# Reordered start of a layer kernel, and two attention answers given earlier in each batch

## The chip, the cores and the metric

The kernel runs on one core of a Trainium2 chip. The metric is the device time of one execution in microseconds (us). TensorE (PE in the profile) multiplies, VectorE (DVE), ScalarE (ACT) and GpSimd (POOL) do the elementwise work, and SyncE (SP) issues the DMAs. The engines run side by side and wait for each other only through semaphores.

## What is computed

```python
xn = _layernorm(x)                       # x: 4 batches x 2048 tokens x 256
# attention part, per batch
Q = l2norm(xn @ Wq.T + bq); K = l2norm(xn @ Wk.T + bk); V = xn @ Wv.T + bv
tailor = 1 / (L + Q^T (sum(K) + EPS))
s = xn + gamma * (sum(V) + Q^T (K V)) * tailor
# feed-forward part: both factors of every product are quantised to FP4, in blocks of 16
h = silu(q4(xn) @ q4(w_gate).T) * (q4(xn) @ q4(w_up).T)     # 704 wide
g = silu(q4(h) @ q4(w_down).T)
out = x + s * g
```

K, V and Q are never formed. The kernel builds the Gram matrix of the normalised rows of a batch, and from it, in a chain of small fp32 products, one 256 x 256 matrix M; s is then xn @ M.

## The kernel before

The 8192 rows go through in 32 pairs of 2 x 128 rows. The program of every engine is a start of its own, then the same iteration p = 0 to 32 written out (`drive`; the middle batches are a hardware loop), then a tail. In iteration p the engines work on different pairs at once. With u the pair number: `x_norm` (ACT) normalises pair u = p + 3 and writes its fp16 high part, `x_low` (POOL) writes the low part, `x_divide` (POOL) divides by the block scales; `x_abs` (ACT) and `x_round` (DVE) quantise pair p + 2; `row_transposes` (PE) and `rows_out` (ACT) turn pair p + 1 around; `gate_up` (PE), `silu` (ACT) and `h_mul` (DVE) form h of pair p in four pieces (j, c); `h_scales`, `h_abs`, `h_round` and others quantise h of pairs p and p - 1; `down_product` (PE) finishes pair p - 2. Ten iterations later PE multiplies the rows by M (`s_half`) beside all this.

The order on an engine is the order in which the calls are written; each call waits on its semaphores and whatever stands behind it waits too.

**The attention chain.** Three tables place its steps in the iterations of a batch: ASKS are PE's steps, ANSWERS are DVE's, COPIES are ACT's. A key is (i, j, place), where i counts the iterations of the batch and i = 0 is the iteration in which its last Gram product is formed. All PE steps write one PSUM bank, G. So the ask "gram1_0" at (0, 1, 2), the last thing that PE does in iteration i = 0, waits until the DVE answer "gram0" has emptied G; and the ask "high_low" at (5, 0, 1) waits until the answer "top" has computed the scalar kap. DVE gives "gram0" at (0, 1, 0), behind `h_round(0)`, `h_mul(1, 0)`, `x_round(2)` and `h_round(1)`, and "top" at (5, 0, 0), behind the first `h_mul` of iteration 5. The last batch has tables of its own (ASKS_END and so on).

**The start.** The gate, up and down weights are quantised in three units z = 0, 1, 2 by the same means as the rows: DVE takes the block maxima, POOL divides (`w_divide`, L485), ACT takes the absolute value (`w_abs`), DVE rounds (`w_round`, L1132 and L1138) and multiplies by the high and by the low scales (`w_scaled`, L1145, two fp16 instructions of up to 128 x 1536; the second raises `wlod`). PE then turns unit 0 and unit 1 around (`gate_up_weights`, 11 steps), ACT copies them out (`gate_up_out`), and only after the eleventh copy can `gate_up` of iteration 0 begin. Unit 2 is scaled in iteration 0 and turned in iterations 0 and 1 (`down_transposes`, L1348; `down_out`, L812). Pairs 0, 1 and 2 are normalised and quantised in between. Their transposes for the later product with M are `first_rows(0)` and `first_rows(1)` in the start and part of `row_transposes` in iteration 0. "weights_v" sums the columns of Wv on PE (four fp32 products, L1568) and ACT copies the sum (L605).

In the start POOL's order is: x_rstd, x_low of pair 0, w_divide(0), x_divide of pair 0, w_divide(1), x_rstd and x_low of pair 1, w_divide(2), x_divide of pair 1, x_rstd and x_low of pair 2, x_rstd of pair 3, x_divide of pair 2.

In every iteration ACT does `x_norm(p)` before `silu(p, 0, 0)`.

Of the kernel before, what the change touches and what calls it, by code (L numbers as in the profile page):

```python
# [26 lines left out]
F16 = mybir.dt.float16  # L27
BF16 = mybir.dt.bfloat16

P = 128  # L30
# [40 lines left out]
def build(nc, x, Wq, bq, Wk, bk, Wv, bv, gamma, w_gate, w_up, w_down, out):  # L71
# [3 lines left out]
    with ExitStack() as ctx:  # L75
# [178 lines left out]
        def spread_in_order(ap, blks):  # L254
# [5 lines left out]

        ASKS = {(-2, 1, 2): "gram0_0", (-1, 0, 1): "gram0_1", (-1, 1, 1): "gram0_2", (6, 1, 2): "gram0_0", (0, 0, 1): "gram0_3",
                (0, 1, 2): "gram1_0", (1, 0, 0): "gram1_1", (1, 0, 2): "turn", (2, 0, 0): "t1q", (2, 0, 2): "t1k",
                (2, 1, 2): "norms", (3, 0, 2): "raw", (3, 1, 2): "tailor", (4, 0, 2): "product", (4, 1, 2): "top",
                (5, 0, 1): "high_low"}
        ANSWERS = {(0, 1, 0): "gram0", (1, 0, 1): "gram1", (1, 1, 0): "turn", (2, 1, 0): "squares",
                   (3, 0, 0): "norms", (4, 0, 0): "tailor", (4, 0, 3): "scale", (4, 1, 0): "product", (5, 0, 0): "top", (5, 0, 2): "high_low"}
        COPIES = {(2, 0, 1): "t1q", (3, 1, 0): "raw"}

# [187 lines left out]
        def _(pool):  # L456
# [62 lines left out]
            x_rstd(-2)  # L519
            x_low(-2, 0)  # L520
            w_divide(2)
            x_divide(-2, 0)
            x_rstd(-1)
            x_low(-1, 1)
            x_rstd(0)
            x_divide(-1, 1)
# [53 lines left out]
        def _(act):  # L580
# [16 lines left out]
            def copy(b, step):  # L597
                matrices = G[:, :].rearrange("p (k n) -> p k n", k=KD)
                if step in ("weights_q", "weights_k"):
                    i = int(step == "weights_k")  # L600
                    act.wait_ge(S["a_tr"], i + 1)
                    a.copy((wqT, wkT)[i][:, :, :], matrices).then_inc(S["a_ev"], 1)
                if step == "weights_v":
                    act.wait_ge(S["wvs_mm"], 1)
                    a.copy(wvs[:, :], G[:, 0:D]).then_inc(S["wvs_ev"], 1)  # L605
                if step == "t1q":
                    wait(act, "tq_mm", b + 1)
                    a.copy(t1q[:, :, :], matrices).then_inc(S["tq_ev"], 1)
                if step == "raw":
                    wait(act, "inv_d", b + 1)  # L610
                    wait(act, "raw_mm", b + 1)
                    for m in range(KD):
                        last = a.activation(raw[:, m], matrices[:, m], ACT.Copy, scale=inv[:, 2 + m:3 + m])
                    last.then_inc(S["raw_ev"], 1)
# [152 lines left out]

            def first_rows_out(u):
                for j in range(2):
                    act.wait_ge(S["n_tr"], 2 * u + j + 1)  # L770
                    xn_out(u, j, "n_ev")

            act.wait_ge(S["consts"], 3)
# [13 lines left out]
            w_abs(1)  # L787
            own_basis(1)
            first_rows_out(0)
            copy(0, "weights_q")  # L790
            for r in range(GUR):
                gate_up_out(r)
                if r == 3:
                    x_stats(-1)
                if r == R0 - 1:
                    copy(0, "weights_k")
                    w_abs(2)
                    x_high(-2, 0)
                    x_norm(-1, 1)
                    x_stats(0)  # L800
                    first_rows_out(1)
                if r == R0 + 2:
                    x_abs(-1, 1)
            for j in range(2):
                rows_out(-1, 1, j, False, False)
            copy(0, "weights_v")
            x_high(-1, 1)

# [6 lines left out]
            def iteration(p, k, b=0, i=-1, tail=False):  # L815
# [7 lines left out]
                if i == 3:  # L823

                    wait(act, "gram_d", 2 * b + 2)
                if on["xa"]:
                    x_norm(p, k)
                if on["m"]:
                    silu(p, 0, 0)
                attention(0, 0)  # L830
                down_out(p, 0, 0)
# [469 lines left out]
        def _(pe):  # L1301
# [13 lines left out]
            t.matmul(DS[:, 0:2], ones32[0:2, :], wdiag[:, :], start=True, stop=True).then_inc(S["walld"], 1)  # L1315
            def first_rows(u):
                for j in range(2):
                    pe.wait_ge(S["xhi"], u + 1)
                    pe.wait_ge(S["xlo"], u + 1)

                    wait(pe, "n_ev", 2 * u - 1 + j)
                    norm_transposes(u, j).then_inc(S["n_tr"], 1)

            def gate_up_weights(r):
# [56 lines left out]
            def row_transposes(p, k, j, h_on, n_on):  # L1381
# [9 lines left out]
                if isinstance(p, int) and p == -1:  # L1391
                    pe.wait_ge(S["n_ev"], 4)
                for z in range(4):
# [76 lines left out]
            def ask(b, step):  # L1470
# [81 lines left out]
                if step in ("weights_q", "weights_k"):  # L1552
# [7 lines left out]
                    for k in range(KD):  # L1560
                        for n in range(KD):
                            last = t.transpose(G[:, k * D + n * P:k * D + (n + 1) * P], wqkv[:, w, n, k * P:(k + 1) * P], id32[:, :])
                    last.then_inc(S["a_tr"], 1)
                if step == "weights_v":
                    pe.wait_ge(S["a_ev"], 2)
                    pe.wait_ge(S["w_own"], 2)
# [3 lines left out]

            first_rows(0)
            ask(0, "weights_q")
            for r in range(R0):
                gate_up_weights(r)
            first_rows(1)
            ask(0, "weights_k")
            for r in range(R0, GUR):
                gate_up_weights(r)
            for j in range(2):
                row_transposes(-1, 1, j, False, False)  # L1580
            ask(0, "weights_v")

# [82 lines left out]
```

## Time and profile before

| | |
|---|---|
| time, median of 3 runs | 608.24 us (607.51 to 609.05) |
| profiled execution: its own time | 607.78 us |
| its span, first to last instruction | 605.7 us |
| DVE busy | 559.3 us, 92% |
| PE busy | 549.9 us, 91% |
| ACT busy | 416.0 us, 69% |
| POOL busy | 246.6 us, 41% |
| mean granted TensorE clock | 0.983 |

The table comes from the page of the profiled execution. DVE and PE share the load almost evenly, so a share of busy time does not say which of them holds the end back in a given stretch; that is read from who waits for whom. In a timeline a row has its start, its length, the engine, line and operation, what it writes and reads, and how often; several instructions of one kind in a row are merged. A bracket gives the idle time before it and what ended that.

### The profile page before, as it was taken

What the parts mean: (1) busy time and instruction counts of PE and PEld (TensorE: products, weight loads), DVE (VectorE), ACT (ScalarE), POOL (GpSimd) and SP (SyncE); (2) the same over time, 40 slices, a digit from 0 to 9 for tenths busy, and PEclk for the clock granted to TensorE, in tenths of its full rate; (3) what the DMA queues carried; (4) which work ended last, traced back from release to release, by engine and by line L of the source; (5) the groups of instructions that cost most, each with busy time, mean ns of one, the idle gap of its engine ahead of it and who ended that gap; (6) DMA issues with size and microseconds to landing.
All of it is one profiled execution on the core that took longest, in us unless ns stands there. A gap on an engine that the chain in (4) does not pass through costs nothing. (4 is left out here: it accounts for less than half of the span.)

```text
span 605.7 us, 15173 instructions
## 1 busy us (share of the span) xinstructions
PE 549.9 (91%) x4957; PEld 427.4 (71%) x4957; DVE 559.3 (92%) x1178; ACT 416.0 (69%) x902; POOL 246.6 (41%) x214
## 2 busy tenths in 40 slices
PE   0478899999999999899999989989999999999886
PEld 0345576768776877678887767768887777778775
DVE  7988999999999999989999997999999999987873
ACT  4878788867787777656876767767777677545331
POOL 7533333333342334444442543444243444423136
PEclk9969899999999999989999999999999999999999
DMA  7010000000011001111011111110111111013033
GB/s 247 17 27 28 19 19 18 18 19 19 18 36 36 18 2 54 55 54 52 3 54 54 54 57 55 53 36 20 54 53 54 55 36 37 36 49 124 22 122 140
DMA packets 17488, 29.14 MB, mean 48 GB/s; under 512 B 2688, under 2 KB 4864, under 8 KB 17408
## 3 DMA queue, kind: packets, MB, share of 16 engines
q1 hardware_dynamic: 17408, 28.13, 14.0%
q8 instruction: 44, 0.72, 0.5%
q14 instruction: 36, 0.29, 0.2%
HBM read 19.73 MB, written 8.39 MB: 46 GB/s over the span
## 5 line engine op out<-in xcount | busy, mean ns | idle before, releaser
L1416 PE MATMUL GU<-wgu,xqT 128*128 128x352 f16 x1536 | 254.8, 317 | 5.5 <-DVE h L935 3.1
L1416 PEld LDWEIGHTS GU<-wgu,xqT 128*128 128x128 f16 x1536 | 149.2, 99 | 80.6 <-issue 4.7
L622 ACT ACTIVATE sil<-GU,wkap 128x352 f32<-128x352 f32 x128 | 70.8, 553 | 71.3 <-PE GU L1416 70.3
L541 POOL TENSOR_TENSOR ht<-h,hrr 128x1408 f32<-128x1408 f32 x32 | 82.9, 2589 | 82.5 <-DVE hrr L949 81.0
L1426 PE MATMUL DS<-wdT,hqT 128*128 128x256 f16 x704 | 87.3, 273 | 1.9 <-ACT hqT L629 1.9
L935 DVE SCALAR_TENSOR_TENSOR h<-GU,wkap,sil 128x352 f32<-128x352 f32 x128 | 69.4, 542 | 18.8 <-ACT sil L622 17.6
L504 POOL TENSOR_TENSOR xnat<-xs,xnat 128x510 f16<-128x510 f32 (+1 forms) x32 | 38.7, 1209 | 106.8 <-DVE hq L983 96.7
L983 DVE TENSOR_TENSOR hq<-hg,hs 128x704 f16<-128x704 f16 x128 | 78.9, 657 | 0.9
L1426 PEld LDWEIGHTS DS<-wdT,hqT 128*128 128x128 f16 x704 | 66.7, 98 | 12.0 <-ACT hqT L629 2.3
L494 POOL TENSOR_TENSOR rs<-ve,half 128x2 f32<-128x2 f32 x32 | 23.9, 747 | 114.3 <-DVE ht L972 109.4
L658 ACT ACTIVATE gring<-DS,hun 128x256 f32<-128x256 f32 (+1 forms) x64 | 29.9, 467 | 43.6 <-issue 29.6
L629 ACT COPY hqT<-TR 128x768 f16<-128x768 f16 x64 | 50.9, 796 | 8.4 <-PE TR L1378 7.4
L972 DVE SCALAR_TENSOR_TENSOR ht<-hT,ht 128x1408 f32<-128x1408 f32 x32 | 51.8, 1619 | 2.4 <-ACT hT L671 2.1
L1428 PE MATMUL DS<-wdT,hqT 128*128 128x256 f16 x384 | 52.4, 273 | 0.0
L975 DVE SCALAR_TENSOR_TENSOR hg<-hT,ht 128x1408 f16<-128x1408 f32 x32 | 51.7, 1616 | 0.0
L942 DVE TENSOR_REDUCE ham<-h 128x88 f32<-128x1408 f32 x32 | 51.4, 1607 | 0.0
L1378 PE MATMUL TR<-id,hq 128*128 128x128 f16 x704 | 50.5, 221 | 0.5 <-DVE hq L983 0.5
L511 POOL TENSOR_TENSOR xt<-xs,xrr 128x512 f32<-128x512 f32 x32 | 34.0, 1061 | 37.0 <-DVE hq L983 25.2
L1437 PE MATMUL GU<-Mx,xnT 128*128 128x128 f16 (+1 forms) x552 | 47.7, 223 | 0.0
L1437 PEld LDWEIGHTS GU<-Mx,xnT 128*128 (+1 forms) x552 | 39.7, 98 | 9.6
L1378 PEld LDWEIGHTS TR<-id,hq 128*128 128x128 f16 x704 | 43.4, 99 | 3.3 <-DVE hq L983 1.1
L671 ACT ACTIVATE hT<-ht 128x1408 f32<-128x1408 f32 x32 | 43.8, 1369 | 1.7 <-POOL ht L541 1.3
(163 smaller groups left out, 955.3 us busy)
## 6 DMA issues: line engine op xcount, KB each, us to landing
xin<-in_L_attn_x SPq DMA_DIRECT2D x34, 256.0 KB, 2.8
xe<-in_L_attn_x SPq DMA_DIRECT2D x25, 256.0 KB, 2.8
out<-o SPq DMA_DIRECT2D x25, 256.0 KB, 2.1
algebra<-in_L_ffn_w_down SPq DMA_DIRECT2D x1, 704.0 KB, 6.7
gring<-in_L_ffn_w_up SPq DMA_DIRECT2D x1, 640.0 KB, 5.5
xs<-in_L_attn_x SPq DMA_DIRECT2D x2, 256.0 KB, 4.1
xt<-in_L_attn_x SPq DMA_DIRECT2D x2, 256.0 KB, 4.5
out<-xin SPq DMA_DIRECT2D x2, 256.0 KB, 2.5
```

Of the source, the lines that this page charges most:

```text
L541: g.tensor_tensor(paired(ht[:, 0:2 * I]), paired(h[:, q]), spread(hrr[:, q], 4 * CB), ALU.mult).then_inc(S["ht_d"], 1)
L622: a.activation(sil[:, c], GU[:, c, 0, 0:CH], ACT.Silu, scale=wkap[:, 0:1]).then_inc(S["sil_d"], 1)
L935: v.scalar_tensor_tensor(h[:, k, (2 * j + c) * CH:(2 * j + c + 1) * CH], GU[:, c, 1, 0:CH], wkap[:, 0:1], sil[:, c], ALU.mult, ALU.mult).t ...
L942: v.tensor_reduce(per_block(ham[:, :]), paired_in_order(h[:, q]), AX.X, ALU.max, apply_absolute_value=True).then_inc(S["ham_d"], 1)
L972: v.scalar_tensor_tensor(ht[:, 0:2 * I], hT[:, 0:2 * I], CUT, ht[:, 0:2 * I], ALU.max, ALU.subtract).then_inc(S["hw_d"], 1)
L975: v.scalar_tensor_tensor(hg[:, 0:2 * I], hT[:, 0:2 * I], CUT, ht[:, 0:2 * I], ALU.max, ALU.subtract).then_inc(S["hg_d"], 1)
L983: v.tensor_tensor(paired(hq[:, q, j, at:at + I]), paired(hg[:, j * I:(j + 1) * I]), spread(scales[:, q, j * HB:(j + 1) * HB], HB), ALU.mul ...
L1378: last = t.transpose(TR[:, bank, zz * P:(zz + 1) * P], hq[:, q, j, z * P:(z + 1) * P], id16[:, :])
L1416: last = t.matmul(GU[:, c, m, 0:CH], xqT[:, k, j, 2 * a_ + kc], wgu[:, b_, kc, 2 * m + c], start=(z == 0 and kc == 0), stop=(z == 2 and kc ...
L1426: t.matmul(DS[:, 0:D], hqT[:, j, z], wdT[:, z], start=(z == 0), stop=False)
L1428: last = t.matmul(DS[:, 0:D], hqT[:, j, LOCH + z], wdT[:, NCH + z], start=False, stop=(z == LOCH))
L1437: last = t.matmul(bank, slot[:, j, 2 * a_ + kc], Mb[:, b_, kc, columns], start=(i == 0 and kc == 0), stop=(i == 2 and kc == KD - 1))
```

## The change

- POOL: the third weight division, w_divide(2), first waits until the scaled copies of unit 0 are written (`wlod` at 1). x_low of pairs 1 and 2 goes behind a wait for the last weight rounding (`wgd` at 3), with x_divide of pair 2 behind them.
- PE and ACT: the eight transposes of pair 1 for the product with M and their copy leave the start, become a step "rows_1" that uses the bank G, and are done in iteration 0; "weights_v" leaves the start too, asked at the end of iteration 0 and copied in iteration 1.
- ACT: x_high of pair 2 moves from the end of the start into iteration 0, behind the first silu. In iterations 0 and 1 `silu(p, 0, 0)` comes before `x_norm(p)`.
- DVE, batches 0, 1 and 2: the answer "gram0" moves from (0, 1, 0) to (0, 0, 3), ahead of `h_round(0)`; the answer "top" (kap) from (5, 0, 0) to (4, 1, 2), between `h_scales(0)` and `h_scales(1)` of the iteration before.

```diff
-        ASKS = {(-2, 1, 2): "gram0_0", (-1, 0, 1): "gram0_1", (-1, 1, 1): "gram0_2", (6, 1, 2): "gram0_0", (0, 0, 1): "gram0_3",
+        ASKS = {(-5, 0, 1): "rows_1", (-5, 1, 1): "weights_v", (-2, 1, 2): "gram0_0", (-1, 0, 1): "gram0_1", (-1, 1, 1): "gram0_2", (6, 1, 2): "gram0_0", (0, 0, 1): "gram0_3",
...
-        ANSWERS = {(0, 1, 0): "gram0", (1, 0, 1): "gram1", (1, 1, 0): "turn", (2, 1, 0): "squares",
-                   (3, 0, 0): "norms", (4, 0, 0): "tailor", (4, 0, 3): "scale", (4, 1, 0): "product", (5, 0, 0): "top", (5, 0, 2): "high_low"}
-        COPIES = {(2, 0, 1): "t1q", (3, 1, 0): "raw"}
+        ANSWERS = {(0, 0, 3): "gram0", (1, 0, 1): "gram1", (1, 1, 0): "turn", (2, 1, 0): "squares",
+                   (3, 0, 0): "norms", (4, 0, 0): "tailor", (4, 0, 3): "scale", (4, 1, 0): "product", (4, 1, 2): "top", (5, 0, 2): "high_low"}
+        COPIES = {(-5, 1, 0): "rows_1", (-4, 0, 1): "weights_v", (2, 0, 1): "t1q", (3, 1, 0): "raw"}
...
             w_divide(1)
             x_rstd(-2)
-            x_low(-2, 0)
+
+            pool.wait_ge(S["wlod"], 1)
             w_divide(2)
             x_divide(-2, 0)
             x_rstd(-1)
+            x_rstd(0)
+
+            pool.wait_ge(S["wgd"], 3)
+            x_low(-2, 0)
             x_low(-1, 1)
-            x_rstd(0)
             x_divide(-1, 1)
...
+                if step == "rows_1":
+                    act.wait_ge(S["n_tr"], 3)
+                    a.copy(xnT[:, 1], G[:, :].bitcast(F16).rearrange("p (j z t) -> p j z t", j=2, t=P)).then_inc(S["n_ev"], 1)
...
-                    first_rows_out(1)
...
-            copy(0, "weights_v")
-            x_high(-1, 1)
...
-                if on["xa"]:
+                first = isinstance(p, int) and p < 2
+                if on["xa"] and not first:
                     x_norm(p, k)
                 if on["m"]:
                     silu(p, 0, 0)
+                if isinstance(p, int) and p == 0:
+                    x_high(-1, 1)
+                if on["xa"] and first:
+                    x_norm(p, k)
...
+                if step == "rows_1":
+                    pe.wait_ge(S["a_ev"], 2)
+                    pe.wait_ge(S["xhi"], 2)
+                    pe.wait_ge(S["xlo"], 2)
+                    for j in range(2):
+                        for z in range(4):
+                            last = t.transpose(G[:, :].bitcast(F16)[:, (4 * j + z) * P:(4 * j + z + 1) * P],
+                                               xnat[:, 1, j, z * P:(z + 1) * P], id16[:, :])
+                    last.then_inc(S["n_tr"], 1)
                 if step == "weights_v":
-                    pe.wait_ge(S["a_ev"], 2)
+                    pe.wait_ge(S["n_ev"], 3)
...
-            first_rows(1)
             ask(0, "weights_k")
...
-            ask(0, "weights_v")
```

## Rows read from the trace of the kernel before

**Rows 1.** The page: busy time, share and instructions of each engine

```profile
PE 549.9 (91%) x4957; PEld 427.4 (71%) x4957; DVE 559.3 (92%) x1178; ACT 416.0 (69%) x902; POOL 246.6 (41%) x214
```

**Rows 2.** Timeline of VectorE, start to iteration 1

```profile
19.97 1.21 DVE L1124 SCALAR_TENSOR_TENSOR ws<-y,wall,ws 128x96 f16<-128x96 f32 x1
21.28 4.03 DVE L1145 TENSOR_TENSOR xnat<-hg,ws 128x1536 f16<-128x1536 f16 x2
...
44.92 0.58 DVE L935 SCALAR_TENSOR_TENSOR h<-GU,wkap,sil 128x352 f32<-128x352 f32 x1 [1.99 <-ACT sil L622]
...
57.86 0.58 DVE L935 SCALAR_TENSOR_TENSOR h<-GU,wkap,sil 128x352 f32<-128x352 f32 x1 [1.75 <-ACT sil L622]
...
62.43 1.61 DVE L972 SCALAR_TENSOR_TENSOR ht<-hT,ht 128x1408 f32<-128x1408 f32 x1
```

**Rows 3.** Source line L1145, unit 0 and 2: shortest, median, longest, ns

```profile
L1145 DVE TENSOR_TENSOR xnat<-hg,ws x4: 857/914/3162, 21.3 to 47.1; 128x1536 f16<-128x1536 f16 x2, 128x1408 f16<-128x1408 f16 x2
```

**Rows 4.** Timeline of GpSimd in the start

```profile
18.72 2.35 POOL L504 TENSOR_TENSOR xnat<-xs,xnat 128x510 f16<-128x510 f32 x1 [2.59 <-ACT xnat L724]
21.02 2.60 POOL L485 TENSOR_TENSOR ht<-algebra,y 128x1408 f32<-128x1408 f32 x1
26.61 1.06 POOL L511 TENSOR_TENSOR xt<-xs,xrr 128x512 f32<-128x512 f32 x1 [2.98 <-DVE xrr L906]
```

**Rows 5.** Timeline of ScalarE, iterations 0 and 1

```profile
42.70 1.09 ACT L711 ACTIVATE xs<-xin,x_shift,rs 128x256 f32<-128x256 f32 x2
...
49.10 2.10 ACT L812 COPY wdT<-TR 128x1024 f16<-128x1024 f16 x3 [0.91 <-PE TR L1348]
...
58.40 0.56 ACT L622 ACTIVATE sil<-GU,wkap 128x352 f32<-128x352 f32 x1
...
60.70 1.39 ACT L671 ACTIVATE hT<-ht 128x1408 f32<-128x1408 f32 x1
```

**Rows 6.** Timeline of TensorE: "gram1_0" of batches 1 and 2, "high_low" of 1

```profile
255.45 1.99 PE L1486 MATMUL G<-xnat 128*128 x8 [2.54 <-DVE algebra L1019]
257.24 3.57 PE L1416 MATMUL GU<-wgu,xqT 128*128 128x352 f16 x12
...
334.57 0.66 PE L1550 MATMUL G<-id,mt 128*128 128x128 f32 x4 [0.84 <-DVE kap L1067]
...
396.96 1.88 PE L1486 MATMUL G<-xnat 128*128 x8 [1.61 <-DVE algebra L1019]
```

**Rows 7.** Timeline of TensorE, end of the start and iterations 0 and 1

```profile
37.04 2.02 PE L1568 MATMUL G<-wqkv,ones 128*128 128x256 f32 x4
38.85 5.32 PE L1416 MATMUL GU<-wgu,xqT 128*128 128x352 f16 x24
...
50.32 1.95 PE L1416 MATMUL GU<-wgu,xqT 128*128 128x352 f16 x12
...
54.52 1.95 PE L1416 MATMUL GU<-wgu,xqT 128*128 128x352 f16 x12
```

**Rows 8.** Who VectorE waited for, 255 to 300 us (batch 1)

```profile
DVE h L935 <- ACT sil L622: 2.9, 4, 1.0
```

**Rows 9.** Who VectorE waited for, 396 to 440 us (batch 2)

```profile
DVE h L935 <- ACT sil L622: 1.4, 3, 0.7
```

**Rows 10.** Who VectorE waited for, 120 to 160 us (batch 0)

```profile
DVE ht L972 <- ACT hT L671: 0.6, 1, 0.6
```

**Rows 11.** Who VectorE waited for, 355 to 375 us

```profile
DVE h L935 <- ACT sil L622: 2.5, 1, 2.5
```

**Rows 12.** Windows: busy time by engine, granted TensorE clock, DMA share, GB/s

```profile
32.00:42.00 10.00, 8.06 (x43) 5.81 (x44) 9.72 (x16) 6.47 (x17) 3.07 (x3) 0.50 0.11 29
42.00:52.00 10.00, 7.36 (x63) 4.92 (x62) 7.87 (x21) 7.20 (x17) 3.94 (x5) 1.00 0.10 26
```

**Rows 13.** Timeline of VectorE where "gram0" is answered, batch 1

```profile
249.71 1.62 DVE L972 SCALAR_TENSOR_TENSOR ht<-hT,ht 128x1408 f32<-128x1408 f32 x1
...
254.37 0.41 DVE L1015 TENSOR_SCALAR algebra<-G 128x256 f32<-128x256 f32 x1
```

More of the change, by code:

```diff
@@ L766, in w_kappa @@
                 a.activation(wkap[:, 1:2], wbeta[:, 1:2], ACT.Copy, scale=-1.0 / (HTOP * TIE * TIE)).then_inc(S["wkapd"], 1)
[L768 to L771, printed above, removed]
             act.wait_ge(S["consts"], 3)
@@ L788, in _ @@
             own_basis(1)
-            first_rows_out(0)
+            for j in range(2):
+                act.wait_ge(S["n_tr"], j + 1)
+                xn_out(0, j, "n_ev")
             copy(0, "weights_q")
@@ L1315, in _ @@
             t.matmul(DS[:, 0:2], ones32[0:2, :], wdiag[:, :], start=True, stop=True).then_inc(S["walld"], 1)
[L1316 to L1322, printed above, removed]
             def gate_up_weights(r):
@@ L1391, in row_transposes @@
                 if isinstance(p, int) and p == -1:
-                    pe.wait_ge(S["n_ev"], 4)
+                    pe.wait_ge(S["n_ev"], 2)
                 for z in range(4):
@@ L1563, in ask @@
                     last.then_inc(S["a_tr"], 1)
+                if step == "rows_1":
+                    pe.wait_ge(S["a_ev"], 2)
+                    pe.wait_ge(S["xhi"], 2)
+                    pe.wait_ge(S["xlo"], 2)
+                    for j in range(2):
+                        for z in range(4):
+                            last = t.transpose(G[:, :].bitcast(F16)[:, (4 * j + z) * P:(4 * j + z + 1) * P],
+                                               xnat[:, 1, j, z * P:(z + 1) * P], id16[:, :])
+                    last.then_inc(S["n_tr"], 1)
                 if step == "weights_v":
-                    pe.wait_ge(S["a_ev"], 2)
+                    pe.wait_ge(S["n_ev"], 3)
                     pe.wait_ge(S["w_own"], 2)
@@ L1569, in ask @@
                     last.then_inc(S["wvs_mm"], 1)
-            first_rows(0)
+            for j in range(2):
+                pe.wait_ge(S["xhi"], 1)
+                pe.wait_ge(S["xlo"], 1)
+                norm_transposes(0, j).then_inc(S["n_tr"], 1)
             ask(0, "weights_q")
```

## The prediction

> **What bounds the kernel.** I first read the page. VectorE is busy for 92% of the span and TensorE for 91% [rows 1], so the bound has to be found stretch by stretch. The waits of VectorE do that: where it waits for nothing, its own work sets the end; where it waits for a silu, the chain through TensorE does. The timelines of the start and then of a whole batch show four places that matter to this change.
>
> In the start, VectorE reaches the two scaled copies of weight unit 0 at 21.28 and needs 4.03 us for them [rows 2]. Their single durations are 857 to 914 ns, and one of them takes 3162 ns [rows 3]. GpSimd ran x_low of pair 1 from 18.72 to 21.07 and the third weight division from 21.02 to 23.62 [rows 4]. So VectorE stood still until GpSimd's instruction was over. The small one before them, 96 elements wide, took 1.21 us from 19.97 [rows 2], nearly all of it the tail of x_low.
>
> Between the start and iteration 0, VectorE waits 1.99 us for the first silu [rows 2], since ScalarE put x_norm (from 42.70) in front of it [rows 5]. After the 1.75 us wait at 57.86 [rows 2] VectorE is never short of work for about a hundred us, so what the start wins on VectorE by its first large rounding of h, at 62.43 [rows 2], should last.
>
> In each batch TensorE stops for the answer "gram0". In batch 1 it stops 2.54 us and in batch 2 1.61 us [rows 6]. After the stop of batch 1 the next 12 products take 3.57 us where 12 take 1.95 elsewhere [rows 6, 7]: the clock has dropped. VectorE then waits 2.9 us for silus [rows 8]. In batch 2 it waits 1.4 us [rows 9], in batch 0 0.6 us [rows 10]. After "high_low" TensorE stops for kap, 0.84 us in batch 1 [rows 6], and the next wait of VectorE is 2.5 us at the turn of the hardware loop [rows 11].
>
> **The start, part by part.** *The scaled copies.* With x_low moved away and the division waiting, GpSimd is idle there. The copies return 4.03 less two of 0.9, that is 2.2; the small one returns about 0.9 of its 1.21 (at most the 1.10 in which x_low overlapped it). Unit 0 is ready at 22.2 instead of 25.3, 3.1 earlier.
>
> *What comes behind it.* The third division, 2.60 long, now starts at 22.2 and ends at 24.8; x_divide of pair 1 (1.06, [rows 4]) follows and runs to 25.9. VectorE arrives at the rounding of unit 1 at about 25.0, an instruction that reads two tiles like those that stood still, and I charge it 0.9. If only some kinds of instruction stand still, the charge is 0. I take 0.9, as the row of x_low is the nearest. That leaves 2.1 for unit 1. The Trainium skill (SBUF — State Buffer, "Who interferes with whom") says that a VectorE instruction with two SBUF inputs and a GpSimd instruction that reads SBUF exclude each other for the whole instruction, and that whoever issues first wins. The 3162 ns of the blocked copy agree. By that rule the 0.9 is a real charge and the rule speaks against this order; were the two to share instead, the start would win some 0.5 more.
>
> *Up to iteration 0.* ScalarE loses the two copies for pair 1, and TensorE loses weights_v, which held it for 2.02 us from 37.04, right in front of the first gate_up at 38.85 [rows 7]. With the 2.1 this lets gate_up begin at about 35.2. Its first half takes 3.5 us at the low clock that this stretch has (0.50, [rows 12]), so the silu is done at 39.4. VectorE is through with its start at 40.2 instead of 42.9: the 2.1, and 0.7 since the x_low of pair 2 no longer blocks a rounding. The 1.99 us wait goes. The first h_mul comes at 40.2, 4.7 earlier.
>
> *What is late next.* The two x_low start when the last weight rounding is done, at about 39.1, and take 2.3, then x_divide of pair 2 runs to 42.4. Behind x_low on ScalarE stands x_norm of pair 3, behind x_divide stands x_abs of pair 2, and behind that the second silu, at 43.1. VectorE comes to the scaled copies of unit 2 at 41.6 and stands until 42.4: 0.8 is given back. 3.8 is left.
>
> *rows_1.* Eight transposes on TensorE (0.45 at full clock, by the spacing of those merged rows elsewhere) and a copy of 1024 elements on ScalarE. The three copies of the down weights took 2.10 [rows 5], so one of the large ones is about 0.95. It stands in front of the copies of the down weights, which TensorE waits for before gate_up(0, 1, 1). That one starts at 47.2 instead of 50.32 [rows 7]: 3.1 is left.
>
> *weights_v.* Four products, 2.02 at half clock [rows 7, 12], so 1.0 at full clock, in front of gate_up(1, 0, 0): 52.3 plus nothing else, instead of 54.52 [rows 7]. 2.2 is left.
>
> *The silu ahead of the norm in iteration 1.* ScalarE is free from 52, but now its first task is a silu that can't start before 54.3. x_norm and its two casts (1.6 in all, of which 1.09 is the norm itself [rows 5]) follow it, then x_abs, then silu(1, 0, 1) at 57.05 instead of 58.40 [rows 5]. The copy of weights_v adds 0.3, so h_abs goes from 60.70 [rows 5] to 59.65 and VectorE's rounding from 62.43 to 61.05. **The start wins 1.4.** Bounds: 3.8 if none of what follows iteration 0's first half is on VectorE's path, 0 if one more of these blockings or copies lands on it.
>
> **The batches.** *gram0.* Its two instructions (0.41 and a like one) move ahead of four units of work that begin at 249.71, to be compared with 254.37 [rows 13]. They are done at 250.6. TensorE comes to the ask at 252.9 (255.45 less 2.54, [rows 6]), so no wait is left, with 2.3 to spare. The move itself costs VectorE nothing, as the instructions are the same; it makes one h_mul 0.8 later, whose reader on TensorE is two pieces away. TensorE gains 2.54 and the 1.62 of the slow twelve in batch 1, more than the 2.9 that VectorE waited: all 2.9 is won. In batch 2 the stop is 1.6, more than the 1.4: all 1.4. In batch 0 at most 0.6, and I take it. Lower bounds: TensorE could use up its lead before the waits come, and 0 is won.
>
> *kap.* It is ready 0.84 earlier, and nothing lies between it and the loop's turn for which TensorE waits: 0.8 of the 2.5 there. In batches 0 and 2 VectorE waits for nothing afterwards, so 0. The answer comes behind the large reduction, 1.6 us after TensorE has delivered its input, so it adds no wait. Bounds 0 and 2.5.
>
> Sum: 1.4 + 2.9 + 1.4 + 0.6 + 0.8 = 7.1. The profiled execution took 607.8 in its own time (span 605.7), which gives 600.7. The median of the runs stands 0.4 above it, so 601.1, with 598.5 to 603.5 as this case's own range.
>
> **The rivals.** *A, the whole start is kept* (3.8 instead of 1.4): 598.7. For it: VectorE hardly waits in iteration 0. Against it: TensorE and ScalarE, not VectorE, set gate_up(1, 0, 0).
>
> *B, the stops of TensorE cost nothing where they are removed.* It then meets another limit of its own, and VectorE waits as before. Batches 1 and 2 return at most 1 together: 605.8. For it: TensorE is 100% busy in both stretches, so part of the waits may be its work and not its lateness. Against it: batch 1 had the longer stop and the longer waits.
>
> *C, B with nothing won in the start either*: 607.5, no change.
>
> *D, slower: the low clock lasts.* The clock was at its lower level, 1.2 GHz (0.50), from 32 to 42 and at full level after that [rows 12]. TensorE had been idle from 29 to 33 us, and was busy almost without a break from 36 on when it rose. In the new order it is idle from about 26.3 to 30.2 and has short breaks up to 35.2. If the rise comes later, each gate_up of 12 products costs 3.57 instead of 1.95 [rows 6, 7], 1.6 each, on the chain. It decides from the fifth of these on, 8 us against the 7.1. Seven of them, up to about 60 us, give 612.4. Against it: gate_up now begins 3.6 earlier and gives an unbroken run of 24 products as before. The Trainium skill (TensorE: Matmul & The Clock Gate, "Why this matters for your kernels") warns of idle gaps between bursts of products; the 3.57 [rows 6] agree.
>
> **How the numbers follow.** Forecast 0.52, A 0.16, B 0.17, C 0.08, D 0.07. A difference under 0.3%, 1.8 us, can't be told from none. Faster: the forecast, A and nearly all of B, 0.83. Same: C and the rest of B, 0.10. Slower: D, 0.07. The range goes from 597.8, beyond A by the wider bound of kap, to 606.2, which takes in B.
>
> **What would show it.** The copies of L1145 all at about 0.9 for unit 0; the rounding of unit 1 (L1132, 1280 wide) at 2.3 or so instead of 1.5; the first h_mul near 40; a wait of ScalarE for gate_up before the first silu of iteration 1; the h rounding near 61. Later, no stop of TensorE at gram1_0 and no clock drop behind it, no waits of VectorE for silus in the first iterations behind gram0 of batches 1 and 2, and 1.7 instead of 2.5 at the loop's turn. The prediction is wrong if those waits stay although the stop is gone, or if the clock rises well after 42.

## The result and the profile after

The changed kernel takes 601.77 us (median of 4 runs, 599.99 to 601.82), the kernel before 608.64 on the same chip (4 runs, 607.51 to 609.33). The ratio is 0.988, with a 95% interval of 0.9864 to 0.9897. Forecast were 601.1 us, 597.8 to 606.2 and a chance of 0.83 for faster. The profiled execution took 601.82 us, with a span of 599.7, 6.0 shorter than before.

In this kernel the lines have moved: the scaled copies are L1151, the roundings of the weights L1138 and L1144, `h_mul` L941, the rounding of h L978, `silu` L629, `x_norm` L718, `gate_up` L1414.

The page again first, for the busy times that answer to [rows 1]:

```profile
PE 549.6 (92%) x4957; PEld 426.0 (71%) x4957; DVE 557.2 (93%) x1178; ACT 416.1 (69%) x901; POOL 258.9 (43%) x214
```

VectorE is busy for 2.1 us less. An instruction that another engine holds up counts as busy while it stands still, so the shorter copies of the start are in this. The other 3.9 of the 6.0 us are waiting of VectorE that has gone. To see where, follow one instruction that stands once in each iteration through both traces: VectorE's large reduction of h (128x1408), L942 before and L948 after. It appears 32 times, the last at 569.17 before and 561.64 after. Its start before less its start after is what has been won up to there; such a list is called a ledger below:

| the reduction of | time before | won up to there | what lies since the row above |
|---|---|---|---|
| pair 0 | 53.5 | 3.4 | the start |
| pairs 1 to 5 | 69.9 to 128.4 | 1.6, at the last 1.5 | iterations 0 and 1 |
| pairs 7 to 13 | 161.4 to 258.3 | 2.8 to 3.0 | "gram0" of batch 0 |
| pair 15 | 295.7 | 6.05 | "gram0" of batch 1 |
| pair 21 | 399.8 | 5.8 | kap of batch 1, turn of the loop |
| pair 23 | 435.5 | 7.4 | "gram0" of batch 2 |
| pair 31 | 569.2 | 7.5 | the last batch |
| end of the span | 605.7 | 6.0 | the tail |

The start, on VectorE's timeline, to be held against [rows 2]:

```profile
20.24 0.32 DVE L1130 SCALAR_TENSOR_TENSOR ws<-y,wall,ws 128x96 f16<-128x96 f32 x1
20.66 1.83 DVE L1151 TENSOR_TENSOR xnat<-hg,ws 128x1536 f16<-128x1536 f16 x2
...
25.29 2.23 DVE L1138 SCALAR_TENSOR_TENSOR h<-gring,h 128x1280 f32<-128x1280 f32 x1
...
39.95 0.48 DVE L941 SCALAR_TENSOR_TENSOR h<-GU,wkap,sil 128x352 f32<-128x352 f32 x1
...
41.30 2.44 DVE L1151 TENSOR_TENSOR xnat<-hg,ws 128x1408 f16<-128x1408 f16 x2
...
54.61 0.58 DVE L941 SCALAR_TENSOR_TENSOR h<-GU,wkap,sil 128x352 f32<-128x352 f32 x1 [1.91 <-ACT sil L629]
...
60.79 1.63 DVE L978 SCALAR_TENSOR_TENSOR ht<-hT,ht 128x1408 f32<-128x1408 f32 x1 [0.37 <-ACT hT L678]
```

And GpSimd's, against [rows 4]:

```profile
22.57 2.60 POOL L485 TENSOR_TENSOR ht<-algebra,y 128x1408 f32<-128x1408 f32 x1 [6.16 <-DVE xnat L1151]
25.11 1.07 POOL L511 TENSOR_TENSOR xt<-xs,xrr 128x512 f32<-128x512 f32 x1
...
38.90 2.27 POOL L504 TENSOR_TENSOR xnat<-xs,xnat 128x510 f16<-128x510 f32 x2 [6.44 <-DVE hg L1144]
41.12 1.07 POOL L511 TENSOR_TENSOR xt<-xs,xrr 128x512 f32<-128x512 f32 x1
```

Read the two together. The copies of unit 0 now take 1.83 instead of 4.03, and the division starts as they end. The rounding at 25.29 takes 2.23; where GpSimd is quiet it takes 1.47 (below). The division has ended at 25.17, so what it stands beside is L511, x_divide of pair 1, from 25.11 to 26.18. The copies of unit 2, at 41.30, take 2.44 where two take 1.6 to 1.7, and reach their normal speed when L511 ends at 42.19. These are the 0.9 and the 0.8 of the prediction. The first h_mul stands at 39.95 with no wait before it. Then VectorE meets waits of 1.91 and 1.04 for silus, and the rounding of h comes at 60.79, 1.6 earlier than before.

TensorE in the middle of batch 1, against [rows 6]:

```profile
254.01 1.80 PE L1484 MATMUL G<-xnat 128*128 x8
255.66 1.95 PE L1414 MATMUL GU<-wgu,xqT 128*128 128x352 f16 x12
...
260.84 0.66 PE L1493 MATMUL G<-id,algebra 128*128 128x128 f32 x4 [0.59 <-DVE algebra L1025]
```

The stop at the Gram product is gone, and so is the slow group of twelve (1.95 instead of 3.57). VectorE has no wait for a silu any more in the stretches of [rows 8, 9] and no wait at all in that of [rows 10]. TensorE now waits 0.6 for the next answer, "turn", which stands where it stood.

At the turn of the hardware loop the view of VectorE's waits, 352 to 375 us, against [rows 11]:

```profile
DVE h L941 <- POOL ht L545: 2.8, 1, 2.8
DVE h L941 <- issue: 0.4, 1, 0.4
```

And the tail, on TensorE's timeline and in the windows of TensorE alone (busy time, granted clock, DMA share, GB/s):

```profile
567.34 0.38 PE L1543 MATMUL G<-mtop,ones 128*128 128x1 f32 x2 [1.45 <-DVE mtop L1068]
568.17 1.11 PE L1548 MATMUL G<-id,mt 128*128 128x128 f32 x4 [0.45 <-DVE kap L1073]
569.08 2.52 PE L1424 MATMUL DS<-wdT,hqT 128*128 128x256 f16 x11
```

```profile
566.00:568.00 2.00, 0.38 (x2) 1.00 0.00 0
568.00:570.00 2.00, 1.83 (x9) 0.50 0.00 0
570.00:572.00 2.00, 2.00 (x14) 0.64 0.75 251
```

The groups of twelve and of eleven products that this text follows are always the same ones, so their length shows the clock. After two idle times of TensorE, 1.45 and 0.45 us, the clock falls to its lower level, 1.2 GHz (0.50), and eleven products take 2.52 instead of 1.36. The kernel before had the same idle times at 575 us and kept its clock there:

```profile
574.87 0.38 PE L1545 MATMUL G<-mtop,ones 128*128 128x1 f32 x2 [1.45 <-DVE mtop L1062]
...
576.20 1.36 PE L1426 MATMUL DS<-wdT,hqT 128*128 128x256 f16 x11
```

So the tail gives back 1.5 of the 7.5.

### The profile page after: what moved, and what is told of

It is laid out like the page before. It is cut to its first block and busy times, and to the rows that moved or that the text cites. A ratio compares the mean times of both kernels' runs of the same rounds, so it can differ in the third digit from the quotient of the medians.

```text
span 599.7 us, 15172 instructions
## 1 busy us (share of the span) xinstructions
PE 549.6 (92%) x4957; PEld 426.0 (71%) x4957; DVE 557.2 (93%) x1178; ACT 416.1 (69%) x901; POOL 258.9 (43%) x214
## 5 line engine op out<-in xcount | busy, mean ns | idle before, releaser
L1414 PE MATMUL GU<-wgu,xqT 128*128 128x352 f16 x1536 | 252.6, 315 | 5.5 <-DVE h L941 2.1
L1414 PEld LDWEIGHTS GU<-wgu,xqT 128*128 128x128 f16 x1536 | 148.3, 99 | 79.7 <-issue 3.6
L629 ACT ACTIVATE sil<-GU,wkap 128x352 f32<-128x352 f32 x128 | 70.8, 554 | 59.8 <-PE GU L1414 58.9
L941 DVE SCALAR_TENSOR_TENSOR h<-GU,wkap,sil 128x352 f32<-128x352 f32 x128 | 69.2, 540 | 13.6 <-ACT sil L629 9.7
L504 POOL TENSOR_TENSOR xnat<-xs,xnat 128x510 f16<-128x510 f32 (+1 forms) x32 | 37.0, 1159 | 89.9 <-DVE hq L989 81.6
L978 DVE SCALAR_TENSOR_TENSOR ht<-hT,ht 128x1408 f32<-128x1408 f32 x32 | 51.8, 1619 | 1.9 <-ACT hT L678 1.9
L948 DVE TENSOR_REDUCE ham<-h 128x88 f32<-128x1408 f32 x32 | 51.5, 1608 | 0.0
L511 POOL TENSOR_TENSOR xt<-xs,xrr 128x512 f32<-128x512 f32 x32 | 34.0, 1063 | 26.6 <-DVE hq L989 25.1
```

Of the source, the lines that this page charges most:

```text
L629: a.activation(sil[:, c], GU[:, c, 0, 0:CH], ACT.Silu, scale=wkap[:, 0:1]).then_inc(S["sil_d"], 1)
L941: v.scalar_tensor_tensor(h[:, k, (2 * j + c) * CH:(2 * j + c + 1) * CH], GU[:, c, 1, 0:CH], wkap[:, 0:1], sil[:, c], ALU.mult, ALU.mult).t ...
L948: v.tensor_reduce(per_block(ham[:, :]), paired_in_order(h[:, q]), AX.X, ALU.max, apply_absolute_value=True).then_inc(S["ham_d"], 1)
L978: v.scalar_tensor_tensor(ht[:, 0:2 * I], hT[:, 0:2 * I], CUT, ht[:, 0:2 * I], ALU.max, ALU.subtract).then_inc(S["hw_d"], 1)
L1414: last = t.matmul(GU[:, c, m, 0:CH], xqT[:, k, j, 2 * a_ + kc], wgu[:, b_, kc, 2 * m + c], start=(z == 0 and kc == 0), stop=(z == 2 and kc ...
```

## The experiments

Twelve kernels ran, each beside the kernel before on the same chip; medians of the kernel before were 608.34, 608.75 and 609.18 in the three groups. Where a reading rests on one profile, it is of one execution. The start differs from profile to profile: VectorE's second rounding of weight unit 0, the last instruction ahead of everything that was changed, stands at 17.89 to 19.11. It is at 18.31 in the kernel before and at 18.59 in the change; "shift" below is measured by it. What is won after iteration 1 varies too among profiles with the same order of the start: 0, -0.1, -0.3 and -0.7 for the old one, 1.4, 1.5, 1.6 and 1.8 for the new one. So a single difference there is good to some 0.4 us.

### One part of the change at a time

*gram0_only*: the kernel before with

```diff
-        ANSWERS = {(0, 1, 0): "gram0",
+        ANSWERS = {(0, 0, 3): "gram0",
```

> The kernel before with one edit: the answer gram0 at (0, 0, 3). Theory (the stops of TensorE at gram1_0 were on VectorE's path, as the waits behind them say): VectorE's large reductions shift by 1.2 us in batch 0, 3.2 more in batch 1 and 1.6 more in batch 2, so the last of them comes 6.0 earlier and the time is 602 to 603, ratio near 0.990; if TensorE's clock drops in the tail as it did in the profile of the changed kernel, 1.6 of it goes back. Rival (the start's shift is what made room): well under 4 us earlier, with waits for silus left in batches 1 and 2.

*top_only*: the kernel before with `(4, 1, 2): "top"` instead of `(5, 0, 0): "top"`.

> The kernel before with one edit: the answer top (kap) at (4, 1, 2). The prediction's term: 0.8 us earlier at the turn of the hardware loop. Theory now: 0, since both traces show VectorE's 2.5 to 2.8 us there ending long after the silu was there; the wait is its own queue's, and TensorE's earlier arrival buys nothing. TensorE's stop for kap (0.84) should be gone in either case.

*start_only*: the changed kernel with both answers put back, which leaves all the edits of the start.

> The changed kernel with both answers back where they were: only the start differs from the kernel before. Theory: the large reduction of iteration 1 comes 1.6 us earlier and the shift stays 1.6 to the end, time 606 to 607. Rival (predicted case A): up to 3.4, since the reduction of iteration 0 came 3.4 earlier. Rival (C): no change.

| | median, us | ratio, 95% | won at the last large reduction | span |
|---|---|---|---|---|
| gram0_only | 602.22 (6 runs) | 0.9909 [0.9889, 0.9928] | 5.8 | 599.8 |
| top_only | 607.78 (12 runs) | 0.999 [0.9978, 1.0002] | 1.5 | 604.1 |
| start_only | 606.11 (12 runs) | 0.9966 [0.9956, 0.9976] | 3.5 | 603.9 |

gram0 alone brings 6.1 us by the medians, the start 2.2, and the 0.6 of top_only can't be told from none, as its interval reaches 1.0002. In gram0_only the winnings come in three steps, 1.2 in batch 0, 3.2 in batch 1, 1.6 in batch 2, the same as in the whole change. In start_only they are 1.8 after iteration 1; the rest, 1.65, appears in batch 1, where this edit does nothing. There the profile of before has a drop of the clock [rows 6] that the profile of start_only hasn't. top_only shows the same jump at the same place (from -0.5 to 1.1). All three ledgers hold this 1.65, and it is the profile of before that has the drop; so of the 3.2 of batch 1 only about 1.6 is the stop itself. This also settles the sum: 5.8, 1.5 and 3.5 make 10.8, and with the 1.65 counted once instead of three times 7.5, which is what the whole change wins up to the same row. That the drop comes in some executions of one kernel and not in others is likely, but no kernel was profiled both with and without it.

What kap does at the loop's turn is seen in the waits of top_only, VectorE 350 to 375 us:

```profile
DVE h L935 <- PE GU L1437: 2.5, 1, 2.5
DVE h L935 <- issue: 0.4, 1, 0.4
```

The stop of TensorE for kap has gone, and the wait at the loop's turn is the same 2.5 to the tenth. At its own place the move does win a little: the ledger of top_only goes up by 0.13, 0.20 and 0.17 at the reductions of pairs 10, 18 and 26, 0.5 in all, where those of gram0_only and start_only go up by at most 0.02. In batch 1 the time from the reduction to the second h_mul behind it is 4.77 instead of 4.95, with no wait in either: the two instructions of kap cost VectorE less behind the reduction than between two h_muls.

### The order of the start

*no_wait_third_division*: the changed kernel without the first wait.

```diff
-            pool.wait_ge(S["wlod"], 1)
             w_divide(2)
```

> The changed kernel without POOL's wait for the scaled copies of unit 0 ahead of the third weight division; x_low of pairs 1 and 2 stay late. Theory: the division then runs from about 16.4 to 19.0, beside the rounding of unit 0 (two tiles read, f32), and the scaled copies at 20.7 meet no GpSimd instruction: the wait buys nothing, the copies take 1.8 as in the changed kernel, though one rounding of unit 0 may be blocked for up to 1 us. Time within 1 us of the changed kernel. Rival (the wait is what freed the copies): the copies take about 4 again and unit 0 is ready 2 us later, up to 1 us of it in the time.

Measured: 602.72 (4 runs), ratio 0.9902 [0.9885, 0.9919]. The theory fell and the rival's time came. VectorE:

```profile
18.12 1.74 DVE L1143 SCALAR_TENSOR_TENSOR hg<-hT,ht 128x1536 f16<-128x1536 f32 x1
...
20.20 4.08 DVE L1150 TENSOR_TENSOR xnat<-hg,ws 128x1536 f16<-128x1536 f16 x2
...
27.09 1.47 DVE L1137 SCALAR_TENSOR_TENSOR h<-gring,h 128x1280 f32<-128x1280 f32 x1
```

GpSimd, the same stretch:

```profile
15.82 0.20 POOL L497 TENSOR_TENSOR x_shift<-nm,rs 128x2 f32<-128x2 f32 x1
20.01 2.59 POOL L485 TENSOR_TENSOR ht<-algebra,y 128x1408 f32<-128x1408 f32 x1 [3.98 <-DVE hg L1143]
```

GpSimd is done at 16.0 and the division starts at 20.01, when VectorE's second rounding (hg<-hT,ht) is over. The wait before it is not GpSimd being held up: the division writes the tile ht which that rounding reads, and `w_divide(2)` has a wait of its own for it (`wgd` at 1). The expectation had left this wait out. So the division can't come before the copies, only beside them or behind them. Beside them it holds them up, 4.08 for the two, as in [rows 2]; this agrees with the Trainium skill (SBUF — State Buffer, "Who interferes with whom"), that the one that starts first keeps the shared ports for its whole instruction. The rounding of unit 1 is then free, 1.47, but the h rounding comes at 61.80 instead of 60.79, although this profile has its second rounding of unit 0 0.5 earlier. By the profiles the wait in front of the third division is worth 1.0 to 1.5 us. The ratios alone don't show it, as the interval here and that of the change, 0.9864 to 0.9897, overlap; the medians give 0.8.

*wait_alone*: the kernel before with that one line in front of w_divide(2), and x_low(-2, 0) still ahead of it.

> The kernel before with one edit: POOL waits for the scaled copies of unit 0 before the third weight division, x_low of pair 1 stays ahead of it. Theory: the small copy of scales still takes 1.2 (x_low), the scaled copies 1.8 instead of 4.0, and the whole start 2 us earlier there, of which ScalarE's queue and the low clock keep part: 0.5 to 1.5 us off the time. Rival: another thing sets the start's end (transposes of pair 1, weights_v, x_norm ahead of the silu): under 0.3 us.

Measured: 607.04 (12 runs), 0.9974 [0.9962, 0.9985]; 1.7 us by the medians, a little above the 0.5 to 1.5 expected. Its profile wins 0.3 after iteration 1, 0.8 with its shift of 0.47 taken out. The copies take 1.83, but x_low still stretches the instruction before them, which takes 1.21 as in [rows 2], and the first silu is waited for as before, 1.99. Removing the line and adding it both say that it carries a good part of what the start wins. The other edits of the start (x_low behind the roundings, the transposes of pair 1, x_high, the silu first in iteration 0) were not tried one by one.

*norm_first_in_1*: the changed kernel with the old order in iteration 1, x_norm ahead of the silu.

```diff
-                first = isinstance(p, int) and p < 2
+                first = isinstance(p, int) and p < 1
```

> The changed kernel with the silu ahead of the norm in iteration 0 only; in iteration 1 x_norm comes first again. Theory (ScalarE sits idle 1.7 us before that silu and then has x_norm, 1.6 us, on the path to silu(1, 0, 1) and h_abs): the norm fills the idle time and the rounding of h comes about 1 us earlier than the 60.8 of the changed kernel; the time is about 1 us lower than its 601.8. Rival: the silu is what VectorE waits for and the order of the change is right: the same or up to 1 us higher.

*weights_v_later*: the changed kernel with "weights_v" asked at (-4, 1, 1) and copied at (-3, 0, 1), an iteration later.

> The changed kernel with weights_v asked one iteration later, at the end of iteration 1, and copied in iteration 2. Theory (its four products, 1.08 us on TensorE, stand in front of gate_up(1, 0, 0), which ScalarE and then VectorE wait for): the first silu of iteration 1 comes 0.9 us earlier, h_abs about 1.1 earlier, the rounding of h at about 60.0 instead of 60.8, time 0.8 lower than the changed kernel's. Rival: another wait replaces it, under 0.3.

| | median, us | ratio, 95% | gate_up(1, 0, 0) | h rounding |
|---|---|---|---|---|
| the change | 601.77 (4 runs) | 0.988 [0.9864, 0.9897] | 52.03 | 60.79 |
| norm_first_in_1 | 599.34 (5 runs) | 0.9851 [0.9834, 0.9868] | | 60.36 |
| weights_v_later | 599.22 (5 runs) | 0.9848 [0.9831, 0.9865] | 51.16 | 59.63 |

Both medians lie 2.4 to 2.6 below the change's, more than the 1.0 and 0.8 expected. But three of the change's four executions probably have the clock drop of the tail, and neither of these two profiles has it; against filler_in_tail below (600.14), which is the change without that drop, they are 0.8 and 0.9 lower. The ledgers at the last reduction say 8.5 and 9.0 instead of 7.5. norm_first_in_1 is shifted by 0.52 against the change, so its rounding is 0.9 earlier, not 0.4; weights_v_later is shifted by 0.05. ScalarE in norm_first_in_1:

```profile
52.72 1.09 ACT L718 ACTIVATE xs<-xin,x_shift,rs 128x256 f32<-128x256 f32 x2
...
54.52 0.55 ACT L629 ACTIVATE sil<-GU,wkap 128x352 f32<-128x352 f32 x1
...
56.37 0.56 ACT L629 ACTIVATE sil<-GU,wkap 128x352 f32<-128x352 f32 x1 [0.61 <-PE GU L1414]
```

ScalarE in the change:

```profile
54.02 0.56 ACT L629 ACTIVATE sil<-GU,wkap 128x352 f32<-128x352 f32 x1 [1.70 <-PE GU L1414]
54.48 1.08 ACT L718 ACTIVATE xs<-xin,x_shift,rs 128x256 f32<-128x256 f32 x2
```

In the change ScalarE stands idle for 1.70 before the silu and then does x_norm; with the norm first that idle time is filled, and the second silu waits for TensorE and not for the norm. This edit of the change costs about 0.9 in iteration 1. "weights_v" costs 0.9 at gate_up(1, 0, 0), and 1.2 at the rounding, as its copy of 0.37 stands in front of h_abs too.

### The clock drops

*filler_in_tail*: the changed kernel with eight products that nothing reads, in the last batch, behind the last h_mul and ahead of the wait for "top". They add work and change no result.

```diff
+                    if isinstance(b, int) and b == BATCHES - 1:
+                        pe.wait_ge(S["h_d"], 4 * PAIRS)
+                        for z in range(8):
+                            t.matmul(GU[:, 0, 0, 0:CH], xqT[:, 0, 0, 0], wgu[:, 0, 0, 0], start=True, stop=True)
```

> The changed kernel with eight products of 352 columns, whose result nobody reads, ahead of TensorE's wait in the ask top of the last batch, where it idles 1.45 us. Theory (the half clock at 568 to 571 us in the changed kernel's profile, 1.6 us, follows from that idle time and hits some executions only): the clock stays at full level there, and the median falls by up to 1.6 us to about 600.2. Rival: the drop has another origin or was in this one profile alone, the time stays.

Measured: 600.14 (599.47 to 600.30, 5 runs), 0.9854 [0.9839, 0.9868]. TensorE:

```profile
565.66 1.36 PE L1545 MATMUL GU<-wgu,xqT 128*128 128x352 f16 x8
567.28 0.38 PE L1547 MATMUL G<-mtop,ones 128*128 128x1 f32 x2 [0.26 <-DVE mtop L1068]
568.11 0.66 PE L1552 MATMUL G<-id,mt 128*128 128x128 f32 x4 [0.45 <-DVE kap L1073]
568.60 1.36 PE L1424 MATMUL DS<-wdT,hqT 128*128 128x256 f16 x11
```

The idle time of 1.45 is down to 0.26, the clock stays at 1.00 and the eleven products take 1.36. The profile keeps all of its 7.6: the span is 598.1. The five times lie within 0.9 us of each other and at least 1.4 below the three slower ones of the change, as the theory had it.

*filler_at_gram1*: the kernel before, gram0 not moved, with ten such products between the two groups of Gram products in batches 0 to 2, where TensorE waits for "gram0".

```diff
+                    if part == 0 and m == 1 and not (isinstance(b, int) and b == BATCHES - 1):
+                        wait(pe, "g_d", 2 * PB * b + 8)
+                        for z in range(10):
+                            t.matmul(DS[:, D:2 * D], wgu[:, 0, 0, 0, 0:P], wgu[:, 0, 0, 1, 0:D], start=True, stop=True)
```

> The kernel before with ten products of 256 columns, whose result nobody reads, in TensorE's stop ahead of gram1_0 in batches 0, 1 and 2; it first waits for ScalarE's last read of that bank. Theory (of the 3.2 us that batch 1 won in the profile, 1.6 was a clock drop that follows from the stop and hits only some executions): the stop stays, filled, the slow twelve products don't appear, and the profile is up to 1.6 shorter than the kernel before's. Rival: all 3.2 is the stop, nothing changes.

Measured: 608.33 (606.34 to 609.82, 10 runs), 0.9982 [0.9968, 0.9997]. The drop in batch 1 is gone:

```profile
254.53 1.26 PE L1481 MATMUL DS<-wgu 128*128 128x256 f16 x10 [0.71 <-ACT gring L658]
256.38 1.83 PE L1490 MATMUL G<-xnat 128*128 x8 [0.58 <-DVE algebra L1019]
258.07 1.96 PE L1416 MATMUL GU<-wgu,xqT 128*128 128x352 f16 x12
```

and VectorE's wait there, 255 to 300 us, has halved against [rows 8]:

```profile
DVE h L935 <- ACT sil L622: 1.4, 3, 0.7
```

1.5 of the 2.9 was the slow clock, 1.4 the stop. The ledger of this profile shows 1.7 won in batch 1, 0.6 lost in batch 0, where there was no drop to prevent, and a drop in the tail (eleven products in 2.51) that costs 1.5. So the profile is 0.8 longer than the one of before and not shorter, and the median gains 0.9, with an interval that ends at 0.9997. Filling the stop is no substitute for moving the answer.

How often do the drops come? Of the 12 profiles of this case without the filler in the tail, 5 have slow products there (2.52, 2.51, 2.43, 2.35 and 1.97 instead of 1.36): the change and its repetition, start_only, both_in_1 and filler_at_gram1. The kernel before, gram0_only, top_only, wait_alone and three others have none, with the same idle times in front. Both the old and the new order of the start stand on both sides, so no edit explains it. The drop in batch 1 is like it: of the four profiles that have gram0's stop unfilled and unmoved, the kernel before and wait_alone (twelve products in 3.57 and 3.35) have it, start_only and top_only (1.96 each) don't, with stops of 2.53 to 2.56 in all four.

### The better versions, and the change once more

*both_in_1*: the changed kernel with norm_first_in_1 and weights_v_later together.

> The changed kernel with both improvements of iteration 1: x_norm ahead of the silu again, and weights_v one iteration later. Theory: with weights_v gone the silu is ready at 53.1 while the norm would hold ScalarE to 54.0, so most of what the two won alone is the same time on ScalarE; the rounding of h comes at about 59.4, 0.2 to 0.3 earlier than with weights_v moved alone, time about 599.0. Rival: they add up, 1.9 lower than the changed kernel in the profile.

*both_and_filler*: both_in_1 with the filler in the tail.

> The same with the eight unread products ahead of TensorE's wait in the ask top of the last batch. Theory: the clock doesn't drop in the tail in any execution; the median is up to 1.6 lower than without where the drop hits most executions, about 598, and the runs lie closer together. Rival: other drops take its place and the two are the same.

*changed_once_more*: the change itself.

> The changed kernel itself once more, for the spread of its executions: the theory of the tail's clock drop expects two groups, near 600.0 without and near 601.8 with it.

| | median, us | ratio, 95% | h rounding | won at the last reduction | span |
|---|---|---|---|---|---|
| changed_once_more | 601.31 (4 runs) | 0.9869 [0.9851, 0.9887] | 60.90 | 7.4 | 599.9 |
| both_in_1 | 600.66 (5 runs) | 0.9856 [0.9837, 0.9875] | 58.54 | 10.1 | 597.2 |
| both_and_filler | 598.05 (5 runs) | 0.9829 [0.9815, 0.9843] | 58.61 | 10.0 | 595.6 |

The repetition gives the change's result again, the tail drop included. Its four times, 599.75, 600.81, 601.82 and 602.05, are not the two clean groups that were expected. In both_in_1 the rival came, and the two edits add up: the rounding is 2.3 earlier than in the change, of which 0.5 is shift, and 3.9 is won after iteration 1 instead of 1.6. both_in_1 loses 1.6 of it again in the tail in its profile; one of its five executions took 1470.82 us, for which I have no cause, and the median of the other four is 599.98. both_and_filler has no drop and keeps its 10.0. Its five times, 597.73 to 598.85, lie below all four of the change's in that group. It is the best version here, 3.3 us faster than the change beside it.

## Why the prediction was right, step by step

**The start: 1.4 forecast, 1.6 measured.** The intermediate times hold: copies done at 22.2 (22.40), first h_mul 40.2 (39.95), gate_up(0, 1, 1) 47.2 (46.91), gate_up(1, 0, 0) 52.3 (52.03), silu(1, 0, 1) 57.05 (56.80), h_abs 59.65 (59.37), rounding 61.05 (60.79). From the first h_mul on the forecast is 0.25 to 0.3 late and stays so. Counted from the second rounding of unit 0, which came 0.28 later in the change's profile than in the one of before, it is 0.5 to 0.6 late. Both blockings that were charged are there, 2.23 and 2.44 in the rows above. That TensorE sets gate_up(1, 0, 0) and that the norm behind the silu delays the next silu were steps of the sum; weights_v_later and norm_first_in_1 showed each by removing it. What the sum did not ask is what the old order would have given in iteration 1; it would have been 0.9 earlier. Rival A had no chance: of the 5.0 at the first h_mul (44.92 to 39.95), 3.4 was left at the reduction of pair 0 and 1.6 at that of pair 1. Rival C is out with the 0.9966 of start_only, whose interval ends at 0.9976.

**gram0 in batches 1 and 2: 4.3 forecast, 4.8 measured**, and in the form forecast: no stop, no slow twelve, no wait for a silu. Rival B is out. The mechanism has two halves that the prediction had as one: 1.4 of VectorE's 2.9 in batch 1 is the stop, 1.5 the clock, by filler_at_gram1. The second half is only there to be won in executions that have the drop.

**gram0 in batch 0: 0.6 forecast, 1.2 measured.** The term was mis-sized. I read one wait [rows 10]; the same view, 120 to 160 us, has another line, 0.3 for a silu:

```profile
DVE h L935 <- ACT sil L622: 0.3, 1, 0.3
```

The last 0.3 is in no wait of the listing, and I have not found it.

**kap: 0.8 forecast at the loop's turn, nothing measured there.** This is the step that failed, in the words "0.8 of the 2.5 there". It took [rows 11] at their word, that VectorE waits for a silu at the loop's turn. The three engines there, in the kernel before and then in gram0_only:

```profile
362.26 3.11 PE L1416 MATMUL GU<-wgu,xqT 128*128 128x352 f16 x12 [2.19 <-issue]
365.49 0.55 ACT L622 ACTIVATE sil<-GU,wkap 128x352 f32<-128x352 f32 x1 [1.36 <-PE GU L1416]
369.36 0.58 DVE L935 SCALAR_TENSOR_TENSOR h<-GU,wkap,sil 128x352 f32<-128x352 f32 x1 [2.52 <-ACT sil L622]
```

```profile
358.13 1.96 PE L1416 MATMUL GU<-wgu,xqT 128*128 128x352 f16 x12 [2.42 <-issue]
360.20 0.55 ACT L622 ACTIVATE sil<-GU,wkap 128x352 f32<-128x352 f32 x1 [0.42 <-PE GU L1416]
365.01 0.58 DVE L935 SCALAR_TENSOR_TENSOR h<-GU,wkap,sil 128x352 f32<-128x352 f32 x1 [2.51 <-issue]
```

Before, the silu ends at 366.04 and the h_mul that is said to wait for it starts at 369.36, 3.3 us later. In gram0_only the twelve products are quicker and the silu ends 4.3 us before the h_mul, and VectorE waits 2.51 all the same. The listing names a silu before, a GpSimd instruction in the change, a product in top_only and nothing ("issue") in gram0_only and start_only; the wait is 2.5, 2.8, 2.5, 2.5 and 2.5. In the kernel before TensorE and ScalarE stand still for 2.2 and 2.4 us at the same turn, each with "issue" as the reason. So the wait isn't data that a faster answer could bring; each of the three engines has one at the turn of the hardware loop. What in it takes the time was not tested. What kap's move did win is the 0.1 to 0.2 in each batch of top_only, by another way than the forecast's.

**Not foreseen: the tail.** The prediction had no term for what lies behind the last reduction. There a clock drop takes 1.5 in the profile, and probably as much in most of the change's runs: one of its first four took 599.99, the other three 601.75 to 601.82.

The sum was 7.1. The parts measured are 1.6 for the start, 1.2, 3.2 and 1.6 for gram0, some 0.5 for kap at its own places, and 0.6 lost in pieces of up to 0.3, the longer wait at the loop's turn among them: 7.5 at the last large reduction. Less the tail's 1.5 this is the 6.0 of the spans. By the medians the gain is 6.9. So the closeness of 601.1 to 601.77 owes something to luck, in errors that cancel: the start was undervalued by 0.2 and gram0 by 1.1, kap was overvalued by 0.3, and the small losses and the tail were left out. And 1.65 of gram0's part in the profiles is a clock drop that the kernel before need not have had. The prediction's own figures for two bounds are off as well: C, which is B without the start's 1.4, comes to 607.2 and not 607.5, and A with kap at 2.5 to 597.0 and not 597.8. Neither changes the reading.

Rival D did not come about: after the first 24 products of gate_up, which take 5.47 us, each twelve take 1.95, from 41.91 on. The granted clock of the change is 1.00 in the windows from 32 us on, against 0.50 in [rows 12], but that column is not to be trusted there, see the last section.

## What to carry to other kernels

Before a wait's named releaser is believed, look when that instruction ended: if it was long done, as at the turn of this loop, no work on the releaser will shorten the wait. Putting an urgent instruction first only helps if its input is there; a queue that idles in front of it (1.70 us before the silu of iteration 1) should do the other work first. And a long GpSimd instruction costs least beside VectorE instructions that it does not hold up: behind the copies the same 2.6 us of division stood beside a reduction and the small instructions around it and held up none of them, and only the x_divide that follows it cost a rounding 0.8. Beside the copies it had cost 2.2.

## What the runs showed of the hardware

VectorE and GpSimd block each other in both directions, although no semaphore stands between the two instructions. x_low of pair 1 took 2.35 beside VectorE's rounding in [rows 4]; in the change two of its kind take 2.27 together, 1.14 each. wait_alone shows the same, VectorE first and then GpSimd:

```profile
18.78 1.74 DVE L1139 SCALAR_TENSOR_TENSOR hg<-hT,ht 128x1536 f16<-128x1536 f32 x1
20.43 1.21 DVE L1125 SCALAR_TENSOR_TENSOR ws<-y,wall,ws 128x96 f16<-128x96 f32 x1
```

```profile
19.30 2.23 POOL L504 TENSOR_TENSOR xnat<-xs,xnat 128x510 f16<-128x510 f32 x1 [2.71 <-ACT xnat L725]
```

The rounding keeps its 1.74 and x_low, issued at 19.30, loses 1.1 until it ends at 20.52; then the small instruction waits for x_low to end at 21.53.

Not every VectorE instruction is held up. In the change the division runs on GpSimd from 22.57 to 25.17, and VectorE's six instructions in that time, a reduction of 128x512 and two of statistics of 128x256 among them, take 0.69, 0.19, 0.35, 0.69, 0.25 and 0.75. In the kernel before the like six begin at 25.24, with GpSimd idle until 26.61, and take 0.68, 0.19, 0.35, 0.69, 0.25 and 0.75.

The clock drop after a short stop seems to be a matter of chance from execution to execution; that one and the same kernel has it and has it not was not profiled. With the same idle times of 1.45 and 0.45 us in front, eleven products took 1.36 in seven profiles and 1.97 to 2.52 in five. It costs 1.5 to 1.7 us each time, and products that nobody reads, put into the stop, kept the clock up in all three profiles that had them at the place looked at.

The column of the granted clock can miss a slow stretch. The change's page of windows gives 1.00 for 35 to 39 us:

```profile
35.00:37.00 2.00, 1.59 (x6) 1.00 0.03 8
37.00:39.00 2.00, 2.00 (x9) 1.00 0.00 0
39.00:41.00 2.00, 2.00 (x17) 1.00 0.00 0
```

while the 24 products of gate_up that run there take this long:

```profile
35.41 5.47 PE L1414 MATMUL GU<-wgu,xqT 128*128 128x352 f16 x24 [1.06 <-ACT xqT L649]
```

That is as long as before (5.32 from 38.85), when the column stood at 0.50 until 42, and from 37 to 39 us 9 products fit in two microseconds where in the kernel before 7 and 8 do at 0.50 (38 to 42) and 14 at 0.99 (42 to 44). The durations of the products are the better witness.
